# The gates of the first output chunk are made inside the last chunk of the recurrence

## The reference, cut to what matters

```
def step(S, xs):                       # 512 times, for 4 x 16 (batch, head) pairs
    Sk = einsum('bhvk,bhk->bhv', S, k_t)
    S = a_t[..., None] * S - (b_t[..., None] * (Sk - v_t))[..., None] * k_t[:, :, None, :]
    o_t = einsum('bhvk,bhk->bhv', S, q_t)
...
o = (o - mu) * rsqrt(var + 1e-05) * ln_g + ln_b      # over the 128 values of a head
g = sigmoid(x @ Wg.T).reshape(B, T, H, DV)           # x is the normed input
return (o * g).reshape(B, T, H * DV) @ Wo.T
```

## Time and profile before

| what | value |
|---|---|
| time, median of 3 runs | 2640.51 us |
| profiled execution, its own time | 2641.39 us |
| its span, first to last instruction | 2639.7 us |
| mean granted TensorE clock | 0.900 |
| PE busy | 2184.4 us (83%) |
| DVE busy | 1925.4 us (73%) |
| ACT busy | 1276.7 us (48%) |
| POOL busy | 579.4 us (22%) |

### The profile page before, as it was taken

How to read it: one execution, slowest core, us unless ns; L and a number is a source line. 1 busy time by engine, 2 the same in 40 slices (tenths; PEclk the granted TensorE clock), 3 DMA queues, 4 the chain that set the end, 5 groups by cost and what they waited for, 6 DMA issues and landing times.

```text
span 2639.7 us, 61365 instructions
## 1 busy us (share of the span) xinstructions
PE 2184.4 (83%) x21482; PEld 1609.4 (61%) x21482; DVE 1925.4 (73%) x4379; ACT 1276.7 (48%) x2731; POOL 579.4 (22%) x577
## 2 busy tenths in 40 slices
PE   5999999999947878878877787788787763699998
PEld 3445888888836666667666666666566662243443
DVE  5222899999949888888988888898888888132334
ACT  2000687777825445454544544454454540334443
POOL 0000244444522212222222222222222223000000
PEclk9999999999958898898888988888988885799999
DMA  6000377766685555555555554555555544310210
GB/s 240 8 8 10 134 270 268 269 244 245 241 333 173 174 186 186 174 179 188 191 171 183 184 190 165 198 186 164 188 180 187 176 169 136 139 48 32 80 64 24
DMA packets 211170, 434.65 MB, mean 165 GB/s; under 512 B 47153, under 2 KB 160553, under 8 KB 181721
## 3 DMA queue, kind: packets, MB, share of 16 engines
q1 hardware_dynamic: 207880, 420.24, 46.2%
q10 hardware_dynamic: 2976, 10.72, 1.0%
q0 software_dynamic: 48, 0.16, 0.0%
HBM read 295.13 MB, written 136.98 MB: 164 GB/s over the span
## 4 chain that ended last, share of the span: by engine, by line
PE 52%; DVE 21%; issue 13%; ACT 11%; DMA 1%; DVEq 1%; SPq 1%; POOL 0%; ACTq 0%; POOLq 0%
PE PS L1364 10%; DVE arena L960 8%; ACT arena L755 4%; PE PS L1478 4%; PE PS L1505 4%; PE PS L1316 3%; PE PS L1403 3%; PE PS L1266 3%; PE PS L1243 3%; PE PS L1352 3%; PE PS L1391 3%; PE PS L1378 2%; DVE arena L1051 2%; DVE arena L994 2%; PE PS L1491 2%
## 5 line engine op out<-in xcount | busy, mean ns | idle before, releaser
L1266 PE MATMUL PS<-arena 128*128 x2048 | 463.7, 386 | 1.8 <-DVEq L945 0.9
L960 DVE SCALAR_TENSOR_TENSOR arena<-PS,SM,arena 128x256 f32<-128x256 f32 x1152 | 452.9, 477 | 15.5 <-ACT arena L640 15.5
L1266 PEld LDWEIGHTS PS<-arena 128*128 128x128 f32 x2048 | 383.4, 188 | 82.1 <-DVE arena L960 6.5
L1364 PE MATMUL PS<-arena 128*128 128x128 f32 x1920 | 330.9, 325 | 74.4 <-ACT arena L760 73.1
L1364 PEld LDWEIGHTS PS<-arena 128*128 128x128 f32 x1920 | 280.2, 225 | 117.4 <-ACT arena L760 92.4
L567 POOL TENSOR_TENSOR arena<-arena 128x256 f32<-128x256 f32 x128 | 114.8, 897 | 1064.3 <-DVE arena L1066 1064.3
L755 ACT ACTIVATE arena<-arena 128x128 f32<-128x128 f32 x960 | 302.0, 395 | 0.0
L640 ACT ACTIVATE arena<-PS,SM 128x256 f32<-128x256 f32 x384 | 209.9, 565 | 88.9 <-PE PS L1266 84.1
L781 ACT COPY arena<-PS 128x512 f32<-128x512 f32 (+1 forms) x188 | 91.1, 520 | 312.6 <-PE PS L1391 312.5
L769 ACT COPY arena<-PS 128x256 f32<-128x256 f32 x240 | 89.6, 373 | 265.8 <-PE PS L1364 265.0
L1352 PE MATMUL PS<-ident,arena 128*128 128x128 f32 x960 | 177.0, 315 | 26.6 <-ACT arena L755 24.9
(11 more groups left out here) (135 smaller groups left out, 3587.6 us busy)
## 6 DMA issues: line engine op xcount, KB each, us to landing
arena<-g_d SPq DMA_DIRECT2D x126, 1024.0 KB, 5.1
arena<-vas_d SPq DMA_DIRECT2D x124, 384.0 KB, 3.2
vas_d<-arena SPq DMA_DIRECT2D x32, 1024.0 KB, 11.4
kq_d<-arena SPq DMA_DIRECT2D x8, 4096.0 KB, 11.5
arena<-kq_d SPq DMA_DIRECT2D x14, 2048.0 KB, 8.4
arena<-beta_d SPq DMA_DIRECT2D x8, 2048.0 KB, 9.2
kb_d<-arena SPq DMA_DIRECT2D x8, 2048.0 KB, 10.3
vas_d<-arena SPq DMA_DIRECT2D x8, 2048.0 KB, 12.5
```

Of the source, the lines that this page charges most:

```text
L960: nc.vector.scalar_tensor_tensor(acc, raw[:, :, i:i + PT_], CW[:, w, i, hh:hh + 1], acc, ALU.mult, ALU.add).then_inc(job_free if i == TAPS ...
L1266: ins = mm(dst.rearrange("p (b n) -> p b n", b=B), W4[:, w, kt, DH * h:DH * (h + 1)], XNT[:, kt, :, bass.ds(c * PT_ + (HALO - halo), halo ...
L1364: ins = mm(bank(7)[:, 128 * gi:128 * (gi + 1)].rearrange("v (l x) -> v l x", l=NB), STR[:, s % 2, gi, :], KQ[d][:, :, p0:p0 + 2].rearrange ...
```

## The change

The gates of output chunk 0 are made in the last chunk of the recurrence, spread over its blocks by a new table `GATE_AT`; banks 4 to 7 take them. `WGT` and `WO` are loaded at the start of that chunk and `OC` in its block 4. The output stage's tiles are laid out anew so that `WGT` and `GATE` lie over `S` and `Xf[0]`, `WO` over `PT32` and `KBT`, `OC` over `KQ1` and `KB`. `centre` is made behind waits on the stores instead of the wait on `oc_in`.

```diff
+GATE_AT = [[], [0, 1, 2], [3, 4, 5], [6, 7], [8, 9, 10], [11, 12], [13, 14, 15], []]
 # tiles of the output stage
         pos[0] = 0
+        WGT = take(2 * H * DH).rearrange("p (c n) -> p c n", c=2)
+        GATE = take(H * CH).rearrange("p (h n) -> p h n", h=H)
         WO = take(H * D).rearrange("p (h d) -> p h d", h=H)
         OCf = take(CH * H)
-        GATE = take(H * CH).rearrange("p (h n) -> p h n", h=H)
...
-        WGT = take(2 * H * DH).rearrange("p (c n) -> p c n", c=2)
 # SP
             def chunk(n, i, c, nxt, nxt2):
+                if not nxt:
+                    sp.wait_ge(x_read, 1 + n * 16)
+                    sp.dma_start(WGT, ...).then_inc(ld_last, 16)
+                    sp.wait_ge(corr_full, n * 9 + 2)
+                    sp.dma_start(WO, ...).then_inc(ld_wo, 16)
                 for m in range(NB):
+                    if m == 4 and not nxt:
+                        sp.wait_ge(pd_full, d_item(n, ("g4", 1)))
+                        sp.wait_ge(pa_full, a_item(n, ("g0", 1), nxt))
+                        sp.dma_start(OCf..., o_d[0:4]...).then_inc(oc_in, 16)
...
-            sp.dma_start(WGT, ...)
-            sp.dma_start(OCf..., ...)
-            sp.dma_start(WO, ...)
 # ACT, at the end of block m, behind corr_copy(m)
+                    for h in ([] if nxt else GATE_AT[m]):
+                        if h == 0:
+                            act.wait_ge(o_ready, n * NB)
+                        act.wait_ge(gate_psum, h + 1)
+                        nc.scalar.copy(GATE[:, h, :], bank(4 + h % 4)).then_inc(gate_raw, 1)
+                        if h % 4 == 3:
+                            gate_sigmoid(h // 4, h + 1)
...
-            for h in range(H):
-                act.wait_ge(gate_psum, h + 1)
-                nc.scalar.copy(GATE[:, h, :], bank(h % 4)).then_inc(gate_raw, 1)
-            for q in range(4):
-                gate_sigmoid(q, 4 * q + 4)
 # DVE
-            dve.wait_ge(oc_in, 16)
+            for s in range(4):
+                dve.wait_ge(o_stored[s], 32 * NS)
             nc.vector.tensor_scalar(centre, ident[:, :], -1.0 / DH, None, ALU.add)
 # PE, in block m < 7, behind corrections(m)
+                        for h in ([] if nxt else GATE_AT[m]):
+                            if h == 0:
+                                pe.wait_ge(ld_last, 16)
+                                pe.wait_ge(xnT_in, 16)
+                                pe.wait_ge(corr_sub, n * N_SUB + 8)
+                            if h >= 4:
+                                pe.wait_ge(gate_raw, h - 3)
+                            gate(h, 0, 4 + h % 4)
...
-            pe.wait_ge(ld_last, 16)
-            pe.wait_ge(xnT_in, 16)
             pe.wait_ge(corr_sub, N_SUB * NS)
             pe.wait_ge(pt_ready, N_PT * NS - 4)
-            for h in range(H):
-                if h >= 4:
-                    pe.wait_ge(gate_raw, h - 3)
-                gate(h, 0, h % 4)
```

More of the change, by code:

```diff
@@ L426, in chunk @@
             def chunk(n, i, c, nxt, nxt2):
+                if not nxt:
+                    sp.wait_ge(x_read, 1 + n * 16)
+                    sp.dma_start(WGT, wgT.rearrange("(c p) n -> p c n", p=128)).then_inc(ld_last, 16)
+                    sp.wait_ge(corr_full, n * 9 + 2)
+                    sp.dma_start(WO, woT.rearrange("(h p) d -> p h d", p=128)).then_inc(ld_wo, 16)
                 for m in range(NB):
+                    if m == 4 and not nxt:
+                        sp.wait_ge(pd_full, d_item(n, ("g4", 1)))
+                        sp.wait_ge(pa_full, a_item(n, ("g0", 1), nxt))
+                        sp.dma_start(OCf.rearrange("v (s x) -> v s x", s=4), o_d[0:4].rearrange("s v l x -> v s (l x)")).then_inc(oc_in, 16)
                     if m == 2:
@@ L466, in _ @@
             sp.wait_ge(p_ext, 7 * (NS - 1) + 4)
-            sp.dma_start(WGT, wgT.rearrange("(c p) n -> p c n", p=128)).then_inc(ld_last, 16)
-            sp.dma_start(OCf.rearrange("v (s x) -> v s x", s=4), o_d[0:4].rearrange("s v l x -> v s (l x)")).then_inc(oc_in, 16)
-            sp.dma_start(WO, woT.rearrange("(h p) d -> p h d", p=128)).then_inc(ld_wo, 16)
             sp.dma_start(BASEC[:, :, :], base_d.rearrange("(b c t) d -> c t b d", b=B, c=NCH)[0]).then_inc(base_in, 16)
@@ L744, in _, with gate_sigmoid @@
             nc.scalar.nop().then_inc(x_read, 1)
+            def gate_sigmoid(q, count):
+                act.wait_ge(gate_raw, count)
+                g = GATE[:, 4 * q:4 * q + 4, :]
+                nc.scalar.activation(g, g, ACT.Sigmoid).then_inc(gate_ready, 1)
             def chunk(n, i, c, nxt, nxt2):
@@ L1341, in _, with gate @@
                 carried(hf)
+            def gate(h, c, b):
+                for kt in range(2):
+                    ins = mm(bank(b).rearrange("p (b n) -> p b n", b=B), WGT[:, kt, DH * h:DH * (h + 1)],
+                             XNT[:, kt, :, bass.ds(c * 128 + HALO, 128)], start=(kt == 0), stop=(kt == 1))
+                ins.then_inc(gate_psum, 1)
             def chunk(n, i, c, nxt, nxt2):
```

## The result

The changed kernel takes 2592.81 us, the median of five runs (2592.61 to 2593.22), against 2640.51 (2638.33 to 2641.89): a ratio of 0.9819, 95% interval 0.9806 to 0.9832, or 47.7 us less. Forecast were 2594 us and 46.6 us less, so time and sign were right. The profiled execution took 2592.64 us, its span is 2590.9 us.

What follows compares the result with a forecast made beforehand. The seam between recurrence and output stage was taken as 48.6 us of serial waits, the last chunk as DVE's chain; 45.6 + 2.0 - 1.0 = 46.6 us saved, predicting 2594 us, forecast 2590 to 2599 (66%), range 2588 to 2604.

Steps and rivals of the forecast that it cites:

- Part 1, the seam: Between recurrence and output stage: 48.6 us shrinks to 2.2 to 3.8 us, a saving taken as 45.6 us.
- the slow bound: In the seam with PE slow: the variance product starts 3.8 us after the last store's landing.
- The sign of 2 to 4 us between landing and variance product: Trace check at the seam: first variance product (L1500) 2 to 4 us behind the last store's landing.
- Part 2, PE in the last chunk: Gates in PE's holes of the last chunk: change between -5.8 and +11.2 us, taken as -2.0 us.
- the loss of 11.2 us: Last chunk's upper bound: gate groups at half clock overrun holes by 10.2 us, first square held back about 1 us.
- The rival of a PE that stays slow: PE slow throughout the last chunk: only 34.4 us saved, 2606 us, or 2600 at half of it; chance 14%.
- Part 3, ACT: ACT in the last chunk takes 18.2 us more work at no cost; if that failed, some 1 us.
- Part 4, the DMAs: Early loads on SP's queue land with margins of 4 and 6 us before DVE's needs: no cost.
- the allowance: 1.0 us set aside for DMA traffic beside the engines, ACT and late instructions together.
- The rival of a larger gain: Last chunk: PE fast in all blocks, all 5.8 us of waits gone; some 52 us saved, 2588 us; chance 7%.

Runs made afterwards that it cites:

- e1: Changed kernel with its three early loads kept, but all 16 gates and sigmoids back behind the last store; 2634.55 us.
- e2: Changed kernel with the gates' copies in the last chunk, but the four sigmoids and their table load behind the last store; 2597.89 us.
- e5: Changed kernel with the 4 MB load of OC back behind the last store; 2607.14 us.
- e3: Kernel before the change plus two idle matmul calls per head where the changed kernel has its gates, results unused; 2639.02 us.
- e4: Changed kernel with the gates in three groups of 6, 5 and 5 in blocks 1 to 3, none later; 2603.22 us.
- e8: Changed kernel with output work tiles moved, centre made early, gate groups 3, 3, 3, 3, 2, 2, plus idle matmuls at three output-stage seams; 2581.18 us.
- e9: The changed kernel once more, unaltered, on another chip; 2594.03 us.

## Why the prediction was right, point by point

**Part 1, the seam: mechanism right, size 1.5 us off.** From the last store's landing to the first variance product 48.6 us became 4.5 us (2249.70 to 2254.17), outside the stated bounds of 2.2 to 3.8. The chain shows the term that was missing: 0.56 us of issue between `centre` and PE's first centring product, where 0.1 us of signalling stood for the whole way from the landing to PE. That is most of the 0.7 us beyond the slow bound. The other 0.8 us are the choice between the bounds: 45.6 counted on some full clock, and the variance product starts 3.55 us after the first centring product, all of it at a granted clock of 0.50. So 44.1 us were saved here, not 45.6. The sign of 2 to 4 us between landing and variance product was missed by the same 0.5 us. e1, e2 and e5 price pieces of it: 7.7 us for the wait for `WGT`, 4.8 us for the sigmoids, 11.6 us for the load of `OC` had it stayed.

**Part 2, PE in the last chunk: right in its result, not in every step.** Forecast -2.0 us, measured -1.75. The first group ran slow for most of its time (7.86 us against 8.2 worked out) and overran its hole by 1.0 us, but DVE did not wait behind it, so the overrun that was charged in part cost nothing. The later groups of three took 5.42 us. The gain was to come from transposes and corrections that halve together, 2.8 us in block 3 and some 2 us elsewhere, half of it counted. Only the transposes halved (1.07 us against 1.94); the corrections of block 3 ran mostly at half clock (3.43 us against 3.69). The longest wait fell from 2.9 to 1.8 us, all waits together by 2.1 us. That the sum came so near is partly luck: no overrun was paid, and half was a guess. e3 shows the gain with PE's activity alone, e4 the loss where groups do not fit.

The rival of a PE that stays slow falls with the clock of 0.79, but half-clock stretches remained over the corrections and most of the gates of blocks 3 and 5. The Trainium skill, page "TensorE: Matmul & The Clock Gate", section "HAM oscillation — how this bites in real kernels", has bursts between waits start slow. The trace agrees for three of the six groups (7.86, 5.58 and 5.81 us) and not for the three of 5.42 us. The prediction set the loss of 11.2 us beside this rule, which is a PE slow throughout; its own figures for groups that only start slow (1.5, 0.8 and 1.4 us of overrun) give 3.7 us. Neither came.

**Part 3, ACT: right.** In block 2 the table load began at 2201.01 and ACT was through with sigmoid and copies by 2205.2, before the transposes of 2205.45:

```profile
2201.01 1.28 ACT L758 ACT_TABLE_LOAD   x1
...
2204.12 1.05 ACT L836 COPY arena<-PS 128x512 f32<-128x512 f32 x2
```

That is 6.7 us behind the corrections of block 2 (2198.45), at the lower of the two times worked out. e2 shows no gain from taking the sigmoids out.

**Part 4, the DMAs: right, and the allowance was too much.** The landing times of the changed kernel:

```profile
arena<-o_d SPq DMA_DIRECT2D x1, 4096.0 KB, 12.8
...
arena<-wgT SPq DMA_DIRECT2D x1, 2048.0 KB, 7.9
arena<-woT SPq DMA_DIRECT2D x1, 2048.0 KB, 13.4
```

`WGT` was issued at 2167.93 and landed 13 us ahead of the first gate. `OC` took 12.8 us where I had said 10; as in e5, the 10 us held no start, and here a load of 384 KB stood just ahead of it. How the rest divides is not shown. The chunk shows no wait of DVE for a load. The 1.0 us that I had set aside was not spent, as e1 shows (81.33 against 81.38 us).

**What the sum did not contain.** 1.56 us before the last chunk and 1.46 us in the output stage lie in code that did not change; what moved the first of them is not shown. Over the profiled runs here with this same code in front, the last chunk began anywhere from 2165.00 to 2167.84 us; the output stage's length went with the clock at its seams, in the kernels without idle matmuls there from 332.4 to 337.4 us. Some 0.5 of the 1.46 us came at its opening: the fifth norm follows the first by 12.00 us before and by 11.46 in the changed kernel. These two made the profiled execution's saving 48.8 us instead of 45.8. The seam and the chunk alone give 45.8 us against 47.6 forecast ahead of the allowance, and the unspent allowance of 1.0 us covered part of that gap; so the forecast of 46.6 us lies between the steps (45.8) and the medians (47.7), close to both by luck. The rival of a larger gain named the right direction but the wrong place.

## What to carry to other kernels

Work that does not depend on a serial stage can be put into its holes, and each hole is to be measured on the engine that does the work: groups that fitted, or overran by 1 us, cost nothing here; three that overran further made the chunk 9.2 us longer, part of it by way of ACT and of the clock. Here the filling raised TensorE's granted clock in the chunk from 0.55 to 0.79, and e3 shows that this alone gives the 1.8 us by which the chunk got shorter. Once the large waits are gone, look at what the first instruction of the next stage waits for: here it was the landing of stores whose region held the next stage's tiles. Other places for these tiles, with `centre` made ahead, brought the 11.5 us between DVE's last copy and the next stage's first norm to 4.4 us, and a better split of the groups to 2.6 us.

## What the runs showed of the hardware that I had not expected

- Loads of 8 MB beside the recurrence, at a DMA share of 0.62 instead of 0.37, left DVE's busy time (71.16 against 71.19 us) and the chunk's length as they were.
- The clock can fall while PE is busy: PE was busy for 3.35 of 3.35 us with the corrections of block 3, at a granted clock of 0.55. Ahead of them lay a gap of 1.64 us, 8 transposes and a gap of 0.73 us. The 64 corrections took 3.69 us before, 3.43 in the changed kernel, and 2.01 in e4, where the clock held.
- The output stage, with the same code in all kernels but e8, took from 332.4 to 337.4 us, and its length went with the clock's falls at its seams. That is more than the 2 us by which an edit of the last chunk is judged. Differences of that size are read from stretches of the trace here, not from medians.
- Between DVE's 0.24 us instruction and the PE product that waited for it stood 0.56 us in which the profile shows no waiting; the same 0.56 us stand there in e4 and e9. It was the one term that was missing from the seam.
